# A transformer tower on one core: attention scores in 32-row strips, matmul outputs in rotating PSUM banks, zero fill moved between engines, gate bias in bf16, and a new instruction order

## What is computed

```python
h = tokens(x)                          # layernorm(768) @ W + bias, layernorm, positions
h = h + attn0(ln(h))                   # 16 heads of 16, causal, weights rounded to five levels
h = h + tanh(ln(h) @ W1 @ W2 @ W3 + b)
h = h + attn1(ln(h))                   # 16 heads of 16, not causal, q and k biases, head mask
xf = ln(h)                             # mixture of 16 experts, one expert per token
score = softmax(xf @ Wg + bg); gate = max(score); idx = argmax(score)
# the first 76 tokens of each expert go through relu(x @ W1[e] + b1[e]) @ W2[e] + b2[e]
h = h + gate * expert_output
```

## Time and profile before

| | |
|---|---|
| time, 3 runs | 345.68 us median (345.63 to 347.43) |
| time of the profiled execution | 347.61 us |
| its span, first to last instruction | 345.5 us |
| PE busy | 325.3 us (94%) |
| DVE, ACT, POOL busy | 196.3, 168.5, 135.4 us |
| mean granted TensorE clock | 0.972 |

### The profile page before, as it was taken

How to read it: one execution, slowest core, us unless ns; L and a number is a source line. 1 busy time by engine, 2 the same in 40 slices (tenths; PEclk the granted TensorE clock), 3 DMA queues, 4 the chain that set the end, 5 groups by cost and what they waited for, 6 DMA issues and landing times.

```text
span 345.5 us, 8877 instructions
## 1 busy us (share of the span) xinstructions
PE 325.3 (94%) x3254; PEld 237.2 (69%) x3254; DVE 196.3 (57%) x525; ACT 168.5 (49%) x483; POOL 135.4 (39%) x247
## 2 busy tenths in 40 slices
PE   4797999999999999999999999979999999999993
PEld 3575877787888778888788888766455464364461
DVE  4616899764476866685946888850342361361350
ACT  0534983475465666557675566531342441450440
POOL 4117687734344666455645453650003012012012
PEclk9779999999999999999999999969999999999998
DMA  7999900000000035224401024968999998983300
GB/s 229 417 390 415 409 4 8 25 25 13 24 25 12 25 99 170 61 100 128 142 21 54 21 72 148 376 210 276 387 388 387 352 388 318 346 328 127 125 11 13
DMA packets 38234, 61.05 MB, mean 177 GB/s; under 512 B 10591, under 2 KB 29000, under 8 KB 37840
## 3 DMA queue, kind: packets, MB, share of 16 engines
q1 hardware_dynamic: 33912, 51.14, 42.2%
q10 hardware_dynamic: 2632, 7.10, 5.4%
q0 software_dynamic: 1648, 2.24, 1.9%
HBM read 54.21 MB, written 8.48 MB: 181 GB/s over the span
## 4 chain that ended last, share of the span: by engine, by line
PE 81%; DVE 7%; ACT 4%; POOL 4%; issue 2%; DMA 1%; DVEq 0%; POOLq 0%
PE bank L1108 13%; PE bank L1075 12%; PE bank L961 9%; PE bank L1014 6%; PE bank L1030 5%; PE bank L1001 5%; PE bank L991 5%; PE bank L972 5%; PE bank L1086 4%; PE bank L1037 3%; PE bank L1114 3%; PE bank L946 2%; PE bank L1020 2%; PE bank L903 2%; PE bank L937 1%
## 5 line engine op out<-in xcount | busy, mean ns | idle before, releaser
L862 POOL DMA_INDIRECT out<-mid,idx x12 | 11.7, 977 | 98.0 <-DVE mid L1487 98.0
L843 POOL TENSOR_TENSOR mid<-mid,tab 128x608 f32<-128x608 f32 x32 | 38.5, 1209 | 25.8 <-PE bank L991 14.1
L1108 PE MATMUL bank<-early,mid 128*64 128x256 f32 (+1 forms) x448 | 43.7, 381 | 0.0
L1391 DVE TENSOR_REDUCE mx<-bank 102x16 f32<-102x608 f32 x32 | 25.1, 784 | 30.1 <-PE bank L991 29.9
L1268 ACT ACTIVATE mid<-bank,cols 128x64 f32<-128x64 f32 (+1 forms) x128 | 25.9, 333 | 25.1 <-PE bank L1086 25.1
L1075 PE MATMUL bank<-early,mid 128*64 128x512 f32 (+1 forms) x192 | 36.2, 596 | 0.7 <-ACT mid L1251 0.7
L1108 PEld LDWEIGHTS bank<-early,mid 128*64 128x64 f32 (+1 forms) x448 | 25.3, 123 | 15.8 <-issue 2.9
L961 PE MATMUL bank<-xnT,attn 128*128 128x256 f32 (+1 forms) x160 | 34.9, 371 | 0.7 <-DVE attn L1346 0.7
L961 PEld LDWEIGHTS bank<-xnT,attn 128*128 128x128 f32 x160 | 29.0, 190 | 4.4 <-issue 1.3
L827 POOL TENSOR_SCALAR rs<-mv 128x1 f32<-128x1 f32 (+2 forms) x50 | 12.8, 255 | 47.9 <-DVE mv L1306 46.2
L828 POOL TENSOR_TENSOR rs<-rs,mhalf 128x1 f32<-128x1 f32 (+2 forms) x50 | 29.5, 589 | 4.2
(11 more groups left out here) (154 smaller groups left out, 636.2 us busy)
## 6 DMA issues: line engine op xcount, KB each, us to landing
early<-in_w SPq DMA_DIRECT2D x52, 512.0 KB, 8.1
expert_in<-k_empty SPq DMA_DIRECT2D x6, 514.0 KB, 24.6
early<-in_xf SPq DMA_DIRECT2D x4, 768.0 KB, 16.7
early<-in_xt ACTq DMA_DIRECT2D x4, 768.0 KB, 23.3
xnT<-in_w SPq DMA_DIRECT2D x4, 512.0 KB, 8.0
tokens<-in_w SPq DMA_DIRECT2D x4, 512.0 KB, 8.6
attn<-in_w SPq DMA_DIRECT2D x4, 512.0 KB, 8.6
mid<-expert_in SPq DMA_DIRECT2D x6, 257.0 KB, 6.3
```

Of the source, the lines that this page charges most:

```text
L843: eng.tensor_tensor(km[:, n % 2], bc(kT[:, :, n * PCOLS:(n + 1) * PCOLS], 2, 4), bc(bc(quarterm[:, :], 2, PCOLS), 1, KC), ALU.mult).then_i ...
L1108: ins = mm(Yp[m % 2][a * width:(a + 1) * width, 0:DIM], hT[:, m % 2, c, a * width:(a + 1) * width], w2s[e % W2_SLOTS][:, c, :], start=c == ...
L1391: link(eng.tensor_reduce(mxv, sv, AX.X, ALU.max))
```

## The change

1. Scores: `Sp` is now four banks, one for each strip of 32 rows (two heads in each of two parts f). A step has 16 products of 32 rows by 76 columns, in eight tiles of 32 rows by 64 columns of the array. The masked keys have two versions and not four, so `km` writes 304 columns and not 608. The mask in layer 0 is written by 16 bf16 products of 152 columns. The heads are ordered anew in the weights.
2. The ring `G` stays at four banks, and `pt` and `pv` take theirs from it like all others. Their own banks and the semaphores for them are gone. DVE takes the reciprocal of the row sums in two instructions, one for each image of the pair. The single fill of `Op` with ones goes. The position tables stand in the score banks, so the first score step waits for `tokn` of tile 7 (before tile 4).
3. The two zero fills move from POOL's start to ACT, behind its first transfers.
4. The gate bias is split once by DVE into three bf16 terms, which one bf16 product of three rows adds (before one float32 product of one row).
5. `GOAL`, some of `COST`, and with them the orders on all engines are new.

```diff
-GOAL = {"exp": 461.9, "z": -51.1, "xs": 148.7, "tabs": 161.6, "cs": 128.5, ...
+GOAL = {"exp": -152.9, "z": 118.8, "xs": 175.8, "tabs": 62.4, "cs": -284.9, ...
...
+           "pt": "act", "pv": "dve"}      (EMPTIES: pt and pv take a bank of the ring)
...
-        km = km_.rearrange("p (b f h n) -> p b f h n", b=2, f=2, h=4)
+        km = km_.rearrange("p (b f h n) -> p b f h n", b=2, f=2, h=2)
...
-        Sp = bank[0][:, :].rearrange("p (f n) -> p f n", f=2)
-        PTp = bank[1][:, 0:512]
-        Op = bank[2][:, 512:1024]
-        G = [bank[3][:, 0:512], bank[3][:, 512:1024], bank[2][:, 0:512], bank[1][:, 512:1024]]
+        low, high = [ctx.enter_context(nc.psum_tensor(f"{n}_banks", [128, 2048], F32)) for n in ("low", "high")]
+        Sp = low[:, :].rearrange("p (g n) -> p g n", g=4)
+        tables = [added[:, :]] + [low[:, n * DIM:(n + 1) * DIM] for n in range(1, TILES - 2)] + [fv[:, 1, :], added[:, :]]
+        G = [high[:, 512 * b:512 * (b + 1)] for b in range(SLOTS_G)]
...
-            for half in (v3a, v3b):
-                eng.memset(half[:, :, :, :], 0.0).then_inc(zeroed, 1)
...
-                    eng.tensor_tensor(km[:, n % 2], bc(kT[:, :, n * PCOLS:(n + 1) * PCOLS], 2, 4), ...
+                    eng.tensor_tensor(km[:, n % 2], bc(kT[:, :, n * PCOLS:(n + 1) * PCOLS], 2, 2), ...
...
+                    corners = [(g, slice(QROW * g, QROW * (g + 1)), r0, r1, slice(at + a * SEQ, at + a * SEQ + r1 - r0), slice(a * SEQ, (a + 1) * SEQ))
+                               for g in range(4) for a, (r0, r1) in enumerate(((0, BROW), (BROW, PROWS)))]
                     if l == 0:
+                        for part in range(2):
+                            for g, strip, r0, r1, q, key in corners:
+                                mm(Sp[r0:r1, g, 0:4 * SEQ], selb[strip, part, 0:r1 - r0], causb[strip, part, :], start=part == 0, ...
                     for f in range(KC):
+                        for g, strip, r0, r1, q, key in corners:
+                            ins = mm(Sp[r0:r1, g, 2 * f * SEQ:2 * (f + 1) * SEQ], qT[strip, f, q], km[strip, n % 2, f, :, key], ...
...
                 elif kind == "pt":
                     pe.wait_ge(p_exp, m)
-                        pe.wait_ge(pt_ready, m - 1)
+                    ps, full = take(uses[(kind, l, n)])
...
                 elif kind == "pv":
-                    pe.wait_ge(pt_ready, m)
+                    emptied(pe, uses[("pt", l, n)])
-                        pe.wait_ge(on_ready, m - 1)
+                    ps, full = take(uses[(kind, l, n)])
...
-                        ins = mm(ps[0:rows(n), 0:EXP], ones[0:1, 0:rows(n)], bgB[0:1, :], start=False, stop=True)
+                        ins = mm(ps[0:rows(n), 0:EXP], onesb[0:3, 0:rows(n)], gate_bf[0:3, 2, :], start=False, stop=True)
...
+            act.wait_ge(consts, 1)
+            for half in (v3a, v3b):
+                eng.activation(half[...], ones[0:KROWS, 0:1].to_broadcast([KROWS, half_images * 3 * 6 * VW]), ACT.Copy, scale=0.0).then_inc(zeroed, 1)
...
+                    (five short DVE instructions behind `wo` that fill gate_bf, then_inc(bias_split, 1))
...
-                    if n == 4:
+                    if n == TILES - 3:
                         ins.then_inc(tables_used, 1)
-                    if n == 7:
-                        eng.memset(Op[0:BROW, 0:HEADS * VW], 1.0).then_inc(tables_used, 1)
...
-                    link(eng.reciprocal(rec[:, n % 2, :], ov[:, :, HD]))
+                    eng.reciprocal(rec[0:SEQ, n % 2, :], ov[0:SEQ, :, HD])
+                    link(eng.reciprocal(rec[BROW:PROWS, n % 2, :], ov[BROW:PROWS, :, HD]))
```

More of the change, by code:

```diff
@@ L85, in constants @@
     head[p, p // HD] = 1.0
[L86 to L89, removed]
+    twin = np.zeros((128, 2), np.float32)
+    twin[p, p % QROW // HD] = 1.0
+    causal, select = np.zeros((128, 2, 4, SEQ), np.float32), np.zeros((128, 2, BROW), np.float32)
     for r in range(128):
-        causal[r, :, :] = np.where(np.arange(SEQ) > q[r], NEG, 0.0)
+        for part in range(2):
+            q = part * QROW + r % QROW
+            if q < SEQ:
+                causal[r, part, :, :] = np.where(np.arange(SEQ) > q, NEG, 0.0)
+                select[r, part, q] = 1.0
     upto = (p[:, None] <= p[None, :]).astype(np.float32)
@@ L107, in constants @@
     slots[0, 2] = EXP * MAIN - MAIN - np.arange(EXP) * (MAIN - LATE)
[L108 removed]
+    mask = np.concatenate([causal.reshape(128, 8 * SEQ), select.reshape(128, 2 * BROW), upto, slots.reshape(128, -1), counts], 1)
     turn = (np.arange(SEQ - 1 + TROWS)[None, :] % SEQ == np.arange(SEQ)[:, None]).astype(np.float32)
@@ L211 @@
 PAIR, TILE, LAYER, EAGER = 6.86, 7.45, 114.2, 1000
-GOAL = {"exp": 461.9, "z": -51.1, "xs": 148.7, "tabs": 161.6, "cs": 128.5, "bs": -12.9, "asum": 199.0, "qs": 24.3, "fB": 247.2,
[4 rows of a table removed]
[L219 to L223, removed]
+GOAL = {"exp": -152.9, "z": 118.8, "xs": 175.8, "tabs": 62.4, "cs": -284.9, "bs": -2.5, "asum": 59.3, "qs": -302.0, "fB": -53.3,
[4 rows of a table added]
+COST = {"pe": {"tb": 1.6, "cs": 0.5, "bs": 4.3, "qs": 0.3, "fB": 1.75, "fW": 1.75, "bo": 0.9, "tok": 2.6, "lnt": 0.23, "qk": 3.47, "v": 0.88, "s0": 0.55, "s1": 0.36,
+               "pt": 0.53, "pv": 0.56, "ot": 0.19, "proj": 0.88, "ffn": 0.88, "log": 0.6, "cnt": 0.25},
+        "dve": {"cw": 2.9, "cs": 2.75, "bs": 0.45, "qs": 0.6, "qz": 1.38, "wo": 2.0, "bo": 0.36, "tok": 1.1, "tokn": 1.03, "lns": 0.58, "s": 1.55,
+                "pv": 0.92, "proj": 0.45, "ffn": 0.36, "ffnr": 0.46, "log": 0.85, "cnt": 0.93},
+        "pool": {"tabs": 6.0, "xs": 0.85, "tok": 1.13, "lns": 1.22, "km": 0.78, "lnx": 0.75, "scat": 1.9},
         "act": {"xs": 2.14, "asum": 2.2, "lnx": 0.52, "fB": 0.5, "fW": 0.5, "lnt": 0.27, "qk0": 0.95, "qk1": 2.0, "v": 0.3, "s": 0.63, "pt": 0.46, "ot": 0.2, "ffn": 0.33, "log": 0.25, "exp": 0.65},
-        "sp": {"v": 6.78, "a1": 0.8, "z": 0.6, "w": 0.7, "b2": 3.4}}
+        "sp": {"v": 5.46, "a1": 0.8, "z": 0.6, "w": 0.7, "b2": 3.4}}
 MODE, SWITCH = {"s": 1, "pv": 2}, 0.09
-HANDOVER = {"pe": 0.22, "dve": 0.1, "act": 0.1, "pool": 0.1, "sp": 1.5}
+HANDOVER = {"pe": 0.22, "dve": 0.1, "act": 0.1, "pool": 0.1, "sp": 1.9}
 ARRIVES = {("dve", "cw"): 5.3, ("pe", "bs"): 5.3, ("act", "asum"): 24.5, ("pool", "tabs"): 3.6, ("dve", "bs"): 10.0, ("pe", "fB"): 35.3,
@@ L236 @@
 EMPTIES = {"cs": "dve", "bs": "dve", "qs": "dve", "fB": "act", "fW": "act", "bo": "dve", "tok": "dve", "lnt": "act", "ot": "act", "proj": "dve",
-           "ffn": "dve", "log": "act", "cnt": "dve", "v": "act", "qk": "act"}
+           "ffn": "dve", "log": "act", "cnt": "dve", "v": "act", "qk": "act", "pt": "act", "pv": "dve"}
 STATS = ("tok", "lns")
@@ L454, in tower @@
     for task in tasks:
-        if task[0] in ("cs", "bs", "qs", "fB", "fW", "bo", "tok", "lnt", "ot", "proj", "ffn", "log", "cnt", "v"):
+        if task[0] in ("cs", "bs", "qs", "fB", "fW", "bo", "tok", "lnt", "pt", "pv", "ot", "proj", "ffn", "log", "cnt", "v"):
             uses[task] = n
@@ L1013, in _ @@
                             value = v3(2 * (m - 1) + a)[:, first:3, j * VW:(j + 1) * VW]
-                            ins = mm(Op[BROW * a:BROW * a + SEQ, h0 * VW:(h0 + 3 - first) * VW], PTs[0:KROWS, n % 2, j, a * SEQ:(a + 1) * SEQ], value, start=True, stop=True)
+                            ins = mm(ps[BROW * a:BROW * a + SEQ, h0 * VW:(h0 + 3 - first) * VW], PTs[0:KROWS, n % 2, j, a * SEQ:(a + 1) * SEQ], value, start=True, stop=True)
+                            if j == 5 and a == 0:
+                                ins.then_inc(full, 1)
                     ins.then_inc(o_full, 1)
                 elif kind == "ot":
-                    pe.wait_ge(on_ready, m)
+                    emptied(pe, uses[("pv", l, n)])
                     ps, full = take(uses[(kind, l, n)])
@@ L1162, in _ @@
             by_token(5)
+            act.wait_ge(consts, 1)
+            for half in (v3a, v3b):
+                eng.activation(half[:, :, :, :].rearrange("p a j n -> p (a j n)"), ones[0:KROWS, 0:1].to_broadcast([KROWS, half_images * 3 * 6 * VW]), ACT.Copy, scale=0.0).then_inc(zeroed, 1)
             done = {}
```

81 lines of the change are left out of this document (42 added, 39 removed), and 8 rows, old and new, of the table GOAL.

## The result

The changed kernel takes **342.86 us** (median of 4 runs, 342.03 to 342.98) against 346.41 for the kernel before beside it: ratio 0.9876, 95% interval 0.9843 to 0.9910. It is faster by 1.2%, where 2.3% were forecast. The direction and the range hold (333 to 345), the size is about half (4.3 us by the ratio, 3.6 by the medians, of 8.1), and it is nearest to rival (c), 341.6. The profiled execution took 342.87 us with a span of 340.9.

The account below looks back on a forecast made before the run. PE, busy all of the time from 56 to 222 us, was taken as the bound. The terms summed as 347.61 - 8.1 + 1.0 + 3.0 - 2.0 - 2.0 = 339.5, times 0.9944 = 337.6 us (2.3% faster), range 333 to 345.

Parts of the forecast that it names:

- rival (c): Half is eaten: first stage gives nothing (+2.0), ring and DVE cost 6 in place of 4; 341.6 us, chance 0.15.
- Part 5: Gate bias on PE's path: ten bias products at 0.12 us, not 0.32; -2.0 us, bounds -0.5 and -2.5.
- Part 6: Zero fills off POOL in the first stage: DVE's multiplication freed, first `tok` 2.0 us earlier; -2.0 us, bounds +1 and -2.9.
- part 3: Second reciprocal on DVE, mostly hidden, felt in the last stretch: +1.0 us, bounds 0 and +2.5.
- part 4: `pt` and `pv` in the ring: 8 to 10 PE waits of 0.3 to 0.4 us; +3.0 us, bounds 0 and +16.
- Part 7: First score step's later condition, `tokn` of tile 7: 0 us as the order is.
- part 8: New orders: no gain in attention, where PE hardly waits; first stage could gain; taken as 0, bounds -3 and +2.
- part 1: Scores in strips on PE: step from 0.67 to about 0.42 us, mask cost kept; 32 steps, -8.1 us, bounds -8.1 and 0.
- Rival (a): Eight tiles give no more than four, score steps stay at 0.67 us: 345.7 us, no change, chance 0.08.
- Part 2: Key mask on POOL: 1.209 us becomes 0.6 to 0.8, but PE does not wait for it; 0.

Follow-up runs that it names:

- c_zero_bias: The kernel before with only the zero fills moved from POOL to ACT and the bf16 gate bias: 339.75 us, 0.9815.
- c_two_recip: c_zero_bias with the division's reciprocal split in two, one for each image: 341.61 us, 0.9856.
- a_wide: The changed kernel with the old 64-row score blocks of four heads, its orders, rotation, fills and bias kept: 348.03 us, 1.0049.
- a_wide_six: a_wide with the two banks left free added to the rotation from the first score step on, orders kept: 347.76 us, 1.0047.
- b_ring_planned: The kernel before with `pt` and `pv` in the ring of four and two reciprocals, order planned anew with old due times: 360.36 us, 1.0408.
- a_old_goal: The changed kernel planned anew with the old due times (GOAL of before), banks' last rows zeroed at the start: 361.41 us, 1.0406.
- a_no_mask: The changed kernel without the causal mask products of layer 0: 339.27 us, 0.9815.
- b_bias: The kernel before with only the gate bias as three bf16 rows, orders kept: 345.13 us, 0.9945.
- a_pool_fill: The changed kernel with its zero fills back on POOL, all else kept: 341.95 us, 0.9868.

## Why the prediction was off

The runs make one path from the kernel before to the changed one. By the ratios, times 346.8 us:

| step | ratio after it | us | forecast |
|---|---|---|---|
| fills on ACT, bf16 bias (c_zero_bias) | 0.9815 | -6.4 | -4.0 (parts 5, 6) |
| second reciprocal (c_two_recip) | 0.9856 | +1.4 | +1.0 (part 3) |
| rotation and new orders (a_wide) | 1.0049 | +6.7 | +3.0 (parts 4, 7, 8) |
| strips (the changed kernel) | 0.9876 | -6.0 | -8.1 (part 1) |
| sum | | -4.3 | -8.1 |

Each ratio is known to about 0.3%, so each step to about 1.5 us at worst: the second reciprocal is not clear of nothing, the others are.

**The step that failed is part 4, with part 8: the rotation at +3.0 us and its order at 0.** It measured 6.7, and in this kernel the mechanism was not the one named. The prediction had waits for banks to be emptied, 8 to 10 of them; the changed kernel's trace has none, and a_wide_six gives PE two banks more and gains nothing. Nor do `pt` and `pv`, which joined the ring, take longer: from each one's start to the next step's they are 38.9 us in all in c_two_recip and 39.4 in a_wide. That leaves the new order, whose `qk`, `lnt` and `cnt` steps are longer by 2.8, 1.9 and 1.5 us in the same traces. It is argued, and not shown, that the ring of four forces such an order: rotation and order were never run apart. Waits for banks are real where the plan fits the ring badly, 5.0 us in b_ring_planned. It is also very uneven: 18.5 us more with the old due times (a_old_goal), part of it in pauses that no wait explains. So the new due times, which part 8 took for worth nothing because "in attention PE hardly waits", are what makes the ring bearable. The premise was read from a kernel whose order had been made for own banks and did not hold for one that had to be planned anew.

Where the 6.7 us lie is shown in part, by the stretches of c_two_recip and then of a_wide, cut at the first score step, the 17th, the last, and near the fillers:

```profile
0.00:52.00 52.00, 44.05 (x190) 35.57 (x194) 33.31 (x90) 31.08 (x65) 26.92 (x71) 0.97 0.81 310
52.00:131.00 79.00, 77.91 (x992) 64.00 (x984) 55.58 (x136) 47.63 (x109) 41.61 (x74) 1.00 0.16 45
131.00:204.00 73.00, 72.91 (x929) 60.16 (x927) 55.35 (x154) 45.23 (x116) 38.82 (x66) 1.00 0.23 72
204.00:225.00 21.00, 18.15 (x211) 14.43 (x200) 19.00 (x92) 12.49 (x46) 10.67 (x22) 0.94 0.81 281
```

```profile
0.00:61.00 61.00, 51.28 (x220) 41.93 (x220) 40.93 (x114) 37.11 (x77) 34.75 (x93) 0.97 0.80 301
61.00:139.00 78.00, 77.25 (x984) 63.11 (x984) 52.94 (x123) 44.60 (x105) 35.74 (x59) 1.00 0.31 98
139.00:207.00 68.00, 67.21 (x927) 54.44 (x929) 52.27 (x132) 42.61 (x105) 36.03 (x61) 1.00 0.16 47
207.00:229.00 22.00, 18.42 (x174) 14.52 (x172) 19.30 (x101) 12.84 (x51) 11.52 (x19) 0.80 0.25 85
```

PE's idle time (length less busy) is 7.9, 1.1, 0.1 and 2.9 us in the first, 9.7, 0.8, 0.8 and 3.6 in the second: 12.0 against 14.8, and 1.8 of the 2.8 lie ahead of the first score step. That step moved from 52 to 61 us. Part 7's later condition is not what it waits for: in the changed kernel `tokn` of tile 7 ends at 56.07 us and the step starts at 60.79, behind a `qk` step for which PE had waited 1.6 us. Whether the condition had a part in that order, no run tells. PE's busy time rises by another 1.1 us, with the granted clock at 0.80 in the last stretch in place of 0.94, where PE had been idle more. These traces differ by 4.1 us in span (341.4 and 345.5), the medians by 6.4, and the profiled run of c_two_recip was itself 1.7 above its median; so some 2 us of the step are not placed.

**Part 1, the strips.** The mechanism was right and the size off: -8.1 forecast, -6.0 measured. Layer 1 did what was said (0.671 to 0.443 us a step, 16 x 0.228 = 3.6). Layer 0 gave 16 x 0.122 = 2.0, because "the mask keeps its cost" was wrong: 0.10 us became 0.20, with sixteen records in place of four. The argument counted columns per tile, and for the mask's own records that is right (0.148 us against 0.146); what it missed is that the second half of the score records behind them is 0.08 us late (a_no_mask). Why, with 48 products and as many loads in one step, no run tells. 3.6 + 2.0 = 5.6 by the steps, 6.0 by the ratio: as far as these tell, all of it on the path, as claimed. Rival (a) is out. The rule of the Trainium skill that was weighed there (TensorE: Matmul & The Clock Gate, Part 3, The mechanism: loads overlap matmuls only with another row group) gave no bound here either; score steps of 0.44 us hold 32 loads of 108 and 131 ns, but on four row groups, so `pv` stays a row that contradicts it. The `qk` step does so too: its 16 loads of 190 ns on all rows (3.0 us) and its 16 products of 256 columns fit in 3.48 us. The same section of the Trainium skill also lets a load run ahead when it targets the background weight buffer; both rows would fit that, and no run here tells.

**Part 2, the key mask:** 0 as forecast; POOL has 49.0 us of idle time before these instructions. **Part 3:** right within the noise. **Part 5:** -1.8 against -2.0, right.

**Part 6, the fills:** the mechanism was right (3.24 to 0.35 us) and the size too small, -5.0 against -2.0 and outside the bound of -2.9. The bound left out that a gap on PE also costs clock: before, the granted clock fell behind the gap and the table products ran at 0.51 (12 to 20 us), in b_bias, which keeps the gap, it fell as well (0.50 in the same stretch), and closing the gap gave 3 us more in those products. DVE's multiplication took 0.35 us beside no fill, 1.68 beside one and 3.24 beside two, and ACT's fills held nothing of DVE: six DVE instructions, the first four of them beside the second fill, took 2.44 us, as in the kernel before. The lock between GpSimd and VectorE that the Trainium skill describes (SBUF — State Buffer, Who interferes with whom), held by the one that issued first for one instruction, agrees with the first two; in the third DVE was also shut out by a fill that began 1.48 us after its own start, and that the rule doesn't give. But a_pool_fill shows that in the changed kernel moving the fills is worth nothing: DVE slips in after the first. The 5 us are real as a difference between two arrangements, not as a price of the fills.

So the change came out at -4.3 on this path (-3.6 by its own medians), because 6.7 us of the gains went into the rotation's order. That the range held is luck: part 4 cost 3.7 us more and part 1 gave 2.1 us less than forecast, and part 6, which gave 3.0 us more, made up for most of that. Rival (c), which is nearest in time, has the wrong reasons: its first stage gives nothing (5.0 measured), and its ring and DVE cost 6 (8.1 measured).

What stays open: how good an order for the ring could get, since only two sets of due times ran and they differ by 18.5 us; and whether one planned for six banks would do without the 6.7 us. The old order with six rotating banks, and strips in fewer than four banks, weren't tried.

## What to carry to other kernels

When buffers become shared, the order has to be planned anew, and here that cost more than the waits for buffers: don't take "the engine hardly waits" from a schedule that will be thrown away, and try more than one set of due times before judging. Deliver the parts of a bundle one by one: here two small edits gave more than the whole bundle (6.4 against 4.3 us). A gap on PE near the start can be worth its length plus what the granted clock loses behind it. And time a step with and without its short products: what they cost need not lie in their own records.

## What the runs showed of the hardware

- Eight 32x64 tiles work at once: 32 float32 records of 76 columns in a step of 0.44 us, where 16 of 152 on four quadrants took 0.67. Within a step, eight such records take 0.066 us, four of the wide ones 0.130.
- Sixteen short bf16 products (152 columns) ahead of the 32 score records cost a step 0.20 us, four of 304 columns ahead of 16 wide ones 0.10. Both take 0.15 us themselves; in the first case the last 16 score records take 0.356 us in place of 0.275.
- A DVE multiplication of 128x256 took 0.35, 1.68 or 3.24 us beside no, one or two POOL fills of 1.6 us each. With two fills it came out as 3.24 us or 1.68 us (b_ring_planned), though it started 0.09 us after the first fill both times.
- The granted clock falls behind idle time on PE: after 2.02 us of waiting in the kernel before, to 0.51 over 12 to 20 us. In the eight microseconds ahead of the fillers it is at 0.71 and then 0.50 (the lower level, 1.2 GHz) in the changed kernel, while PE is busy 2.57 and 2.29 of 4 us, the four before them 3.60:

```profile
213.00:217.00 4.00, 3.60 (x28) 2.79 (x26) 3.55 (x22) 2.60 (x11) 2.85 (x6) 1.00 0.33 112
217.00:221.00 4.00, 2.57 (x13) 1.88 (x13) 3.19 (x21) 2.19 (x11) 2.28 (x4) 0.71 0.15 58
221.00:225.00 4.00, 2.29 (x13) 1.73 (x13) 3.21 (x21) 1.84 (x10) 2.09 (x3) 0.50 0.16 60
```
